# Experts written out on ScalarE and the vector engine, with all bounds loaded ahead of the first tile

## What is computed

```python
x = x + tanh(g_xattn[0]) * L0_attention(layernorm(x), ctx)
x = x + tanh(g_ffn[0])   * L0_experts(layernorm(x))
x = x + tanh(g_xattn[1]) * L1_attention(layernorm(x), ctx)
x = x + tanh(g_ffn[1])   * L1_fourier(layernorm(x))
```

```python
topw, sel = top_k(softmax(x @ gate_w.T), 2)
topw = topw / sum(topw)
gu = einsum('th,efh->etf', x, gate_up_w)      # 256 -> 2 x 1024
hact = up * gelu(gate)                        # the two halves of gu
expert_out = einsum('etf,ehf->eth', hact, down_w)   # 1024 -> 256
```

## Time and profile before

| | us |
|---|---|
| median of 3 runs | 1316.13 |
| lowest and highest of the runs | 1311.7, 1317.1 |
| span of the profiled execution (first to last instruction) | 1255.6 |
| median less that span | 60.5 |

### The profile page before, as it was taken

How to read it: one execution, slowest core, us unless ns; L and a number is a source line. 1 busy time by engine, 2 the same in 40 slices (tenths; PEclk the granted TensorE clock), 3 DMA queues, 4 the chain that set the end, 5 groups by cost and what they waited for, 6 DMA issues and landing times.

```text
span 1255.6 us, 35065 instructions
## 1 busy us (share of the span) xinstructions
PE 1159.1 (92%) x11816; PEld 968.8 (77%) x11816; DVE 885.0 (70%) x2697; ACT 570.0 (45%) x1187; POOL 268.5 (21%) x394
## 2 busy tenths in 40 slices
PE   4799999998699998999998999999998999999996
PEld 3678888886488887787887888888886777877774
DVE  4688888897376665757656666776566878778773
ACT  4466666675232422424224242422234666666553
POOL 6024444444310000000000000000014344444310
PEclk9899999998799999999999999999998999999998
DMA  9544444445341221222312222100023222322210
GB/s 282 209 131 153 147 149 152 152 142 179 132 157 45 73 96 41 86 63 64 98 39 80 74 67 88 41 31 31 27 65 95 72 78 82 93 88 77 79 39 17
DMA packets 82755, 119.67 MB, mean 95 GB/s; under 512 B 27325, under 2 KB 52557, under 8 KB 80588
## 3 DMA queue, kind: packets, MB, share of 16 engines
q1 hardware_dynamic: 64172, 60.32, 15.4%
q0 software_dynamic: 12848, 49.05, 11.7%
q10 hardware_dynamic: 5616, 8.78, 1.9%
HBM read 63.81 MB, written 47.58 MB: 89 GB/s over the span
## 4 chain that ended last, share of the span: by engine, by line
PE 77%; DVE 9%; issue 6%; ACT 3%; SPq 2%; ACTq 2%; DMA 1%; DVEq 0%; POOL 0%; POOLq 0%
PE bank L1772 27%; PE bank L1785 14%; PE bank L1599 7%; PE bank L1533 6%; PE bank L1455 5%; PE bank L1475 3%; PE bank L1516 3%; PE bank L1586 3%; PE bank L1518 2%; PE bank L1539 2%; PE bank L1597 1%; PE bank L1610 1%; PE bank L1501 1%; PE bank L1559 1%; DVE bm L1093 1%
## 5 line engine op out<-in xcount | busy, mean ns | idle before, releaser
L1772 PE MATMUL bank<-tiles,we 128*128 128x256 f16 (+1 forms) x3744 | 395.1, 259 | 5.8 <-issue 4.9
L1772 PEld LDWEIGHTS bank<-tiles,we 128*128 128x128 f16 x3744 | 325.9, 98 | 47.1 <-issue 13.3
L947 ACT ACTIVATE tiles<-bank 128x256 f32<-128x256 f32 (+1 forms) x312 | 109.5, 354 | 336.3 <-PE bank L1772 300.4
L1785 PE MATMUL bank<-we,tiles 128*128 128x256 f16 x1608 | 225.5, 274 | 20.7 <-DVE tiles L1385 19.8
L1381 DVE SCALAR_TENSOR_TENSOR tiles<-bank,tiles 128x256 f32<-128x256 f32 (+1 forms) x312 | 119.8, 384 | 164.7 <-ACT tiles L947 161.2
L1785 PEld LDWEIGHTS bank<-we,tiles 128*128 128x128 f16 x1608 | 148.1, 98 | 59.3 <-DVE tiles L1385 33.7
L1533 PE MATMUL bank<-qT,kbd 128*128 128x256 f16 x960 | 150.3, 274 | 2.7 <-issue 2.0
L1093 DVE TENSOR_REDUCE bm<-bank 128x4 bf16<-128x308 f32 x256 | 116.8, 474 | 28.1 <-PE bank L1518 19.9
L1387 DVE TENSOR_TENSOR tiles<-tiles 128x256 f16<-128x256 f32 (+1 forms) x312 | 121.1, 388 | 11.8 <-DVE tiles L1385 1.3
L471 DVE TENSOR_TENSOR pr<-pr 128x512 f16<-128x512 f32 x160 | 108.3, 681 | 25.2 <-ACT pr L809 21.5
L1533 PEld LDWEIGHTS bank<-qT,kbd 128*128 128x128 f16 x960 | 92.1, 98 | 19.6 <-issue 3.1
(11 more groups left out here) (198 smaller groups left out, 1654.0 us busy)
## 6 DMA issues: line engine op xcount, KB each, us to landing
expert_out<-zeros SPq DMA_DIRECT2D x16, 896.0 KB, 4.2
wes<-in_guT POOLq DMA_DIRECT2D x9, 1024.0 KB, 5.1
tiles<-expert_in SPq DMA_DIRECT2D x29, 256.0 KB, 2.6
pr<-in_guT POOLq DMA_DIRECT2D x7, 1024.0 KB
yg<-in_dnT POOLq DMA_DIRECT2D x7, 1024.0 KB
expert_out<-tiles ACTq DMA_DIRECT2D x28, 256.0 KB, 2.1
expert_in<-zeros POOLq DMA_DIRECT2D x8, 640.0 KB, 13.1
xin<-in_x SPq DMA_DIRECT2D x16, 256.0 KB, 2.8
```

Source lines behind the costliest of these rows:

```text
L947: act.activation(ge[:, fc % 2, 0:n * P], bank[1 + fc % 3][:, 0:n * P], ACT.Gelu, scale=INV).then_inc(s.gelu, 1)
L1772: last = pe.matmul(bank[1 + fc % 3][:, half * S:half * S + w * P], gate_up[:, par, c, i, col:col + P], xT[:, j, c, 0:w * P], start=n == 0, ...
L1785: last = pe.matmul(bank[4 + t][:, 0:D], act16[:, fc % 4, i, t * P:(t + 1) * P], we[:, par, 2, j, fc * D:(fc + 1) * D], start=fc == 0 and n ...
```

## The change

ScalarE loads 25 entries into registers once (nine bounds, eight ends of full tiles, eight first rows of results), behind its waits for `credits_given` and `table_zeroed` and ahead of `x_hi(0)`. VectorE loads 17, behind its wait for `tiles_counted` and ahead of `x_low(0)`. The loop over pairs goes; both engines have the eight experts written out one after the other, with the same tiles and the same two inner loops.

```diff
@@ ScalarE @@
+            bound = [act.value_load(tbl[0:1, e:e + 1], min_val=4 if e else 0, max_val=TILES)
+                     for e in range(E + 1)]
+            end = [act.value_load(tbl[0:1, 2 * E + 1 + e:2 * E + 2 + e], min_val=3, max_val=TILES - 1)
+                   for e in range(E)]
+            offset = [act.value_load(tbl[0:1, 3 * E + 1 + e:3 * E + 2 + e], min_val=0,
+                                     max_val=OUT_ROWS - SHORT * P) for e in range(E)]
+
             def expert(e, par):
-                t0 = act.value_load(tbl[0:1, bass.ds(e, 1)], min_val=0, max_val=TILES - 4)
-                t1 = act.value_load(tbl[0:1, bass.ds(e + 1, 1)], min_val=4, max_val=TILES)
-                tw = act.value_load(tbl[0:1, bass.ds(e + (2 * E + 1), 1)], min_val=3, max_val=TILES - 1)
-                first = act.value_load(tbl[0:1, bass.ds(e + (3 * E + 1), 1)], min_val=0,
-                                       max_val=OUT_ROWS - SHORT * P)
+                t0, t1, tw, first = bound[e], bound[e + 1], end[e], offset[e]
                 expert_tile(e, t0, par, 0, first, t0, tw)
...
             x_hi(0)
-            with act.Fori(0, E // 2 - 1) as pair:
-                expert(pair * 2, 1)
-                expert(pair * 2 + 1, 0)
-            expert(E - 2, 1)
+            for e in range(E - 1):
+                expert(e, (e + 1) % 2)
             expert(E - 1, None)
@@ VectorE @@
             def expert(e, par):
-                t0 = dve.value_load(tbl[0:1, bass.ds(e, 1)], min_val=0, max_val=TILES - 4)
-                t1 = dve.value_load(tbl[0:1, bass.ds(e + 1, 1)], min_val=4, max_val=TILES)
-                tw = dve.value_load(tbl[0:1, bass.ds(e + (2 * E + 1), 1)], min_val=3, max_val=TILES - 1)
+                t0, t1, tw = bound[e], bound[e + 1], end[e]
...
             dve.wait_ge(s.tiles_counted, 1)
+            bound = [dve.value_load(tbl[0:1, e:e + 1], min_val=4 if e else 0, max_val=TILES)
+                     for e in range(E + 1)]
+            end = [dve.value_load(tbl[0:1, 2 * E + 1 + e:2 * E + 2 + e], min_val=3, max_val=TILES - 1)
+                   for e in range(E)]
             x_low(0)
-            with dve.Fori(0, E // 2 - 1) as pair:
-                expert(pair * 2, 1)
-                expert(pair * 2 + 1, 0)
-            expert(E - 2, 1)
+            for e in range(E - 1):
+                expert(e, (e + 1) % 2)
             expert(E - 1, None)
```

## The result

The changed kernel takes 1298.89 us (median of 6 runs, 1295.57 to 1301.55) where the kernel before takes 1313.13 (6 runs, 1309.45 to 1317.1). The ratio, formed from the single runs, is 0.9879, with a 95% interval of 0.9857 to 0.9902: 15.9 us less, between 12.9 and 18.8. The two medians alone give 0.9892, or 14.2 us, which lies inside that interval.

A forecast was written before the change was run, and what follows sets the result against it. TensorE, busy in 92% of the span, was taken as the bound. Terms -17.7 + 0.2 = -17.5 us took the span from 1255.6 to 1238.1; with 60.5 around it, 1298.6 us, range for 8 in 10 1294.5 to 1305.0.

The forecast's parts named there:

- The boundaries: First tiles of experts 1 to 7 become as short as second tiles: -17.7 us, at least 13.4 gained.
- The waits of 5 us at `down`: Sign in the profile after: TensorE's two waits of about 5 us at `down` are gone.
- L947 loads its table once: Sign on ScalarE: the table load at L947, 1.28 us at each branch back, comes only once.
- the clock stays at 1.00: Sign: TensorE's granted clock stays at 1.00 through the first tiles of experts 2 and 4.
- the second tile was no floor: At boundaries, the second tile, 16.53 us, was taken as what the first becomes; at most 17.7 us gained.
- TensorE's waits for the split product: Sign among the experts: TensorE's waits for VectorE's split at L1385 fall from 19.8 to some 3 us.
- The moved loads: Loads ahead of the first tile, hidden by its transfer and turning and TensorE's loads: +0.2 us, bounds 0 to +6.1.
- The first rival: ScalarE's sequencer cannot pass waiting L917, L920, L923; loads end 6.1 us late before the first tile: 1304.5 us, chance 0.11.
- The two rows against that rival: VectorE's six memsets within 0.1 us and TensorE's loads from 325.8, cited against loads starting late ahead of the first tile.
- The time around the span: 60.5 us outside the profiled span, added to the predicted span of 1238.1 us.
- Slow entry of new code: Rival at boundaries: entering code forwards costs 2.5 us too, seven first tiles each 1.0 us longer: 1305.6 us, chance 0.07.
- Crowding: Rival ahead of the first tile: loads of three engines slow each other, at three times 1324 us, chance 0.03.

The follow-up runs named there:

- second profile of before: The kernel before, unchanged, run and profiled once more: span 1310.7 us, the run 1312.28 us.
- the last kernel: Changed kernel with the loads of ScalarE, VectorE and TensorE spread over the experts' tiles instead of ahead of the first tile: 1288.59 us, ratio 0.9801.

## Why the prediction was right, and where it was not

**The number was right, and the mechanism for most of it.** Forecast 1298.6, measured 1298.89.

*The boundaries: right, somewhat too small.* The waits of 5 us at `down` are gone, L947 loads its table once, the clock stays at 1.00 in the first tiles of experts 2 and 4 (where the prediction speaks of 0.93 at expert 2 and 1.00 at the others, the profile has 0.93 at expert 4 as well). The term was -17.7 us; the first tiles of experts 1 to 7 lost 133.38 - 114.84 = 18.5 against the same profile and 20.3 against the second one, where expert 4's tile is longer. First tiles came out below second ones (16.39 against 16.52), so the second tile was no floor. Expert 0's first tile, left out of the prediction, lost another 1.0 us (19.06 to 18.08). That is the clock and not the loads: TensorE is busy all through it in both (19.03 and 18.05 us), at a mean granted clock of 0.86 and 0.90. The kernel with eight more loads, which has none behind `x_hi(0)` either, takes 19.12 us at 0.85, and the last kernel, which has three there, 18.07 at 0.91. What decides between the two was not found. TensorE's waits for the split product are 4.4 us, not 3.

*The moved loads: wrong, and this is the step that failed.* The prediction put them at +0.2 us, "hidden by the transfer and turning of the first tile and by TensorE's loads". They cost 5.4. The first rival, given 0.11, is what happened, in place and size: it had the loads begin behind the waiting L917, L920 and L923 and take 13.9 us, with 6.1 to pay. They began with L920 and took 383.06 to 396.93, 13.87 us. Most of the difference to 6.1 is that the start of L920 decides, half a microsecond before L923. The two rows against that rival were misread. VectorE's six memsets within 0.1 us are operations for the engine, and that such operations may be handed over ahead says nothing of loads, which the sequencer runs itself. TensorE's loads at 325.8 came right behind the start of the first of its sixteen products at L1749, which had waited for L917's result (324.96 and 0.60) and started at 325.62; the other fifteen needed nothing more. The loads did not run ahead of a wait, they followed the end of one.

*The time around the span: wrong, without consequence.* The prediction added "60.5 us around it" to the span. There are 1.6 us around it in the second profile of before and in the changed kernel; most of the rest is that the first layer was 48.6 us shorter in the profiled execution than in the second one. A sum of differences against the median did not feel this, but a term read from the first layer would have.

*Why the number came out all the same.* Against the second profile the expert stage gave 4.6 us more than the forecast's 17.7 (2.6 of it at the boundaries, 1.0 at expert 0 by the clock, the rest spread over other tiles) and the start took 5.2 us more than its 0.2. The two errors cancel: -16.9 in the table against the forecast's -17.5. That is luck. The timed difference of -15.9 agrees with the sum within its interval. There is luck in the starting point too: the median of three runs of before, 1316.13, stood 3 us above the median of six, and without that the forecast would have been 1295.6 and not 1298.6.

*The other rivals.* Slow entry of new code: refuted, no first tile of experts 1 to 7 is over 16.47 us. Crowding: refuted. TensorE's 16 loads ran until 389.6 and VectorE's 17 from 384.6 to 394.8, and ScalarE's L965 beside them took 281 ns in the median, L969 275; the earlier trace rows have 274 and 275. From the first to the last start ScalarE's 25 take 13.3 us here (383.1 to 396.4) and 13.3 in the kernel where VectorE loads nothing meanwhile (384.5 to 397.8).

## What to carry to other kernels

Code moved out of a loop lands somewhere: ask what releases the instruction just ahead of it in its own stream, because that is when it starts if the sequencer runs it itself, as it does a load of a register, whatever its own operands need. Of three engines that meet at a boundary only the one that ends last is worth shortening; here ScalarE's change gave 17.0 of 20.3 us at the boundaries and VectorE's alone nothing; once ScalarE's was in, VectorE's was worth the remaining 3.3. Loads of bounds cost nothing where the engine waits anyway, one or two at a time inside a tile, and their full length where they stand in a row ahead of the first piece of work.

## What the runs showed of the hardware

What a sequencer runs itself (a wait instruction, a load of a register) did not run here while an operation ahead of it on its engine still waited for a semaphore. The wait instruction at L932 ran at 383.0, when L920 began, though what it asked for had been there since 333.1; moved ahead, it ran at 377.2, when L917 began, having stood directly behind it for the 8.77 us that L917 waited. Once the semaphore is there, the sequencer does go on: L923 started only at 383.49, and L932 and the first load had begun by 383.1.

This does not say that nothing is handed over to a waiting engine. TensorE, same place, kernel after:

```profile
L1750 PEld LDWEIGHTS bank<-yg,pr x16: 186/190/190, 379.2 to 382.4; 128*128 128x128 f32 x16
L1756 PEldq EVENT_SEMAPHORE  x1: 51/51/51, 379.3 to 379.3; - x1
```

The first of the sixteen weight loads waited for L917 and began at 379.24. The wait instruction behind all sixteen and their products, 31 further instructions, ran 0.07 us later. That is 2 ns for each of them, where the shortest instruction of a sequencer in these rows takes 17; so they had most likely been handed over while the first still waited, and the wait instruction alone was held back. On ScalarE one operation, L923, stands between L920 and L932, which ran 8 ns after L920's start. "Engine Queue Depths" in "Advanced Engine Details and Errata" of the Trainium skill gives ScalarE and VectorE a queue of 8, by which I had argued against the first rival. No row here measures that depth, and none speaks against it; what the rows show is that loads of registers do not profit from it.

Going back over a long piece of code costs far more than the branch. The branch itself takes 0.06 us, and the next instruction comes some 2.5 us later. With the loop gone, experts 2 and 4 lost their holes, and expert 2, entered forwards, is as short as expert 1. "Instruction fetch mechanics" in "Runtime: NRT & Kernel Launch" of the Trainium skill says that a taken branch out of the pages being held has to fetch its target first. The trace agrees as far as it goes: some 2.5 us on ScalarE at the loop over pairs, nothing that shows at the inner loop. The runs don't part the size of the code from its distance.

The first layer takes between 338 and some 390 us in the same code. TensorE is busy 28 us longer in the long execution, at a mean clock of 0.90 instead of 0.96, and idle some 20 us longer; what sets this off was not looked into and stays open. A profile whose span lies 60 us below the timed runs, where 1.6 us lie around a span, does not show what those runs did.
